# Cross attention's scores and maxima on two row tiles of the TensorE array

## The reference, cut to what matters

```python
x = _layernorm(x + attn(x))                       # self attention, 16 heads of 16
# cross attention: x (32, 112, 256) over ctx (32, 375, 256)
q1, q2 = (q[..., :8], q[..., 8:])                 # each of the 16 heads has two halves of 8
k1, k2 = (k[..., :8], k[..., 8:])
a1 = softmax(q1 @ k1.T / sqrt(8)); a2 = softmax(q2 @ k2.T / sqrt(8))
attn_output = (a1 - lam * a2) @ v                 # times 0.8, out projection
x = _layernorm(x + output)
x = x + moe(x)                                    # 8 experts, top 2, then a last norm
```

## Time and profile before

| | |
|---|---|
| median of 3 runs | 1861.12 us |
| the profiled execution's own time | 1862.62 us |
| its span, first to last instruction | 1860.7 us |
| TensorE busy (modelled) | 1629.8 us, 88% |
| VectorE busy | 1153.1 us, 62% |
| ScalarE busy | 915.8 us, 49% |
| mean granted TensorE clock | 0.954 |
| cross attention, first to last score matmul | 479.4 to 1183.8 us |

### The profile page before, as it was taken

How to read it: one execution, slowest core, us unless ns; L and a number is a source line. 1 busy time by engine, 2 the same in 40 slices (tenths; PEclk the granted TensorE clock), 3 DMA queues, 4 the chain that set the end, 5 groups by cost and what they waited for, 6 DMA issues and landing times. The chain is left out here.

```text
span 1860.7 us, 46590 instructions
## 1 busy us (share of the span) xinstructions
PE 1629.8 (88%) x17724; PEld 1223.2 (66%) x17724; DVE 1153.1 (62%) x2648; ACT 915.8 (49%) x2168; POOL 747.5 (40%) x928
## 2 busy tenths in 40 slices
PE   4899999995999999999999998579999999999950
PEld 2666666663566666666665665368888888888840
DVE  5566666662888887788777888434444444444424
ACT  2344444443466666666666665434444444444423
POOL 6343343322755666765775576301111101111116
PEclk9999999997799999999999999779999999999985
DMA  6666666644444445555554453356555566666637
GB/s 174 186 188 172 177 187 176 181 112 97 136 139 138 131 125 145 145 140 136 147 166 124 132 150 98 127 199 238 224 220 222 223 228 237 238 238 228 220 88 184
DMA packets 204149, 317.11 MB, mean 170 GB/s; under 512 B 60600, under 2 KB 170840, under 8 KB 203928
## 3 DMA queue, kind: packets, MB, share of 16 engines
q1 hardware_dynamic: 188280, 247.16, 44.5%
q0 software_dynamic: 15648, 66.97, 10.2%
HBM read 225.84 MB, written 87.89 MB: 169 GB/s over the span
## 5 line engine op out<-in xcount | busy, mean ns | idle before, releaser
L1165 DVE TENSOR_REDUCE cross_mx<-cross_bank_max 112x2 f32<-112x750 f32 x512 | 460.7, 933 | 119.1 <-PE cross_bank_max L1245 116.4
L996 ACT ACTIVATE cross_probs<-cross_bank_score 125x448 f32<-125x448 f32 x768 | 406.5, 545 | 241.9 <-PE cross_bank_score L1235 238.9
L1556 PE MATMUL experts_bank_h<-experts_x_hi,w 128*128 128x256 f16 x2240 | 373.3, 274 | 1.4 <-DVE experts_x_lo L1477 1.4
L1556 PE MATMUL experts_bank_h<-experts_x_lo,w 128*128 128x256 f16 x1120 | 306.6, 274 | 0.0
L1514 DVE TENSOR_TENSOR experts_hid<-experts_bank_h,experts_gated 128x256 f32<-128x256 f32 x280 | 118.6, 424 | 285.5 <-ACT experts_gated L1453 285.4
L1235 PE MATMUL cross_bank_score<-cqst,ckst 97*125 97x448 f16 x768 | 283.9, 371 | 4.8 <-ACT cross_probs L996 2.4
L1245 PE MATMUL cross_bank_max<-ckst,cqst 96*112 96x375 f16 x1024 | 258.8, 335 | 28.2 <-DVE cross_mx L1165 21.2
L1427 POOL DMA_INDIRECT y<-experts_y,experts_dest_i x70 | 67.2, 960 | 510.1 <-ACT experts_y L1465 499.4
L1556 PEld LDWEIGHTS experts_bank_h<-experts_x_hi,w 128*128 128x128 f16 x2240 | 220.0, 98 | 27.7 <-DVE experts_x_lo L1477 1.8
L1261 PE MATMUL cross_bank_out<-cross_probs,cross_val 125*32 125x112 f32 x6144 | 202.0, 264 | 0.1
L1453 ACT ACTIVATE experts_gated<-experts_bank_h 128x256 f32<-128x256 f32 x280 | 107.5, 384 | 189.9 <-PE experts_bank_h L1556 185.5
(11 more groups left out here) (216 smaller groups left out, 2746.9 us busy)
## 6 DMA issues: line engine op xcount, KB each, us to landing
w<-w_halves SPq DMA_DIRECT2D x35, 3072.0 KB, 11.7
cross_ew<-in_experts POOLq DMA_DIRECT2D x32, 768.0 KB, 5.5
w_halves<-cross_ew_half POOLq DMA_DIRECT2D x32, 768.0 KB
ckst<-cross_k SPq DMA_DIRECT2D x96, 187.5 KB
cross_v<-front_v SPq DMA_DIRECT2D x24, 531.2 KB
cross_val<-cross_v SPq DMA_DIRECT2D x32, 398.4 KB
front_src<-in_ctx_t SPq DMA_DIRECT2D x24, 500.0 KB, 8.9
experts_rows<-routed SPq DMA_DIRECT2D x35, 260.0 KB, 6.3
```

The source lines that it names most:

```text
L996: nc.scalar.activation(probs[:, e % PROBS], bank_score[e % 2][0:SC, 0:4 * T], ACT.Exp, scale=CROSS_SCALE).then_inc(probs_ready, 1)
L1165: nc.vector.tensor_reduce(mx[:, b % nb, 2 * n:2 * n + 2], bank_max[n % 2][0:T, :, 0:S], AX.X, ALU.max).then_inc(max_read, 1)
L1556: last = nc.tensor.matmul(bank_h[f % 4][:, mat * BLOCK:(mat + 1) * BLOCK], w13(p, wh, mat, k, f), xt[:, p, k], start=n == 0, stop=n == len ...
```

## The change

Each group's 96 rows are cut in two tiles of 64 rows of the array: head j of the two has its 3 terms x 16 channels = 48 rows at partitions 64 j to 64 j + 47, and a row of ones (in `kst`) or of negated maxima (in `qst`) at 64 j + 48. `qst` has now 2 x 112 columns for a group in place of 4 x 112. A score part becomes two matmuls of 49 rows x 224 columns, one on each tile, both into the same bank. A maxima matmul has 48 rows and 375 columns as before. The pair of maxima of the odd n is cut: its tile-1 half moves to part k = 1, its tile-0 half stays at k = 2. The second score of each part waits on a new semaphore `half_full` until the first is complete. The maxima's order in `mx` is kept by `units_of`. The keys come in 6 transfers of 16 channels in place of 3 of 32, and each row of maxima in two transfers of 8 units in place of one of 16.

```diff
-        sp.dma_start(kst[32 * term:32 * term + 32, p],
-                     cross_k[half].rearrange("(g r) n -> r g n", r=32)[:, :, bass.ts(b, S)]).then_inc(sem, 16)
+        src = cross_k[half].rearrange("(g j r) n -> j r g n", j=2, r=16)
+        for j in range(2):
+            row = 64 * j + 16 * term
+            sp.dma_start(kst[row:row + 16, p], src[j, :, :, bass.ts(b, S)]).then_inc(sem, 16)
...
-            row = 32 * term + 8 * i
-            sp.dma_start(qst[row:row + 8, p, :, i * T:(i + 1) * T], src[i, :, :, bass.ts(b, T)]).then_inc(sem, 16)
+            row = 64 * (i // 2) + 16 * term + 8 * (i % 2)
+            sp.dma_start(qst[row:row + 8, p, :, (i % 2) * T:(i % 2 + 1) * T], src[i, :, :, bass.ts(b, T)]).then_inc(sem, 16)
...
-                pool.memset(ckst[STACK:STACK + 1], 1.0).then_inc(early_ones, 1)
+                pool.memset(ckst[:], 1.0).then_inc(early_ones, 1)
...
-                    sp.dma_start(qst[STACK:STACK + 1, p, 4 * h:4 * h + 4, :].rearrange("o g (i t) -> o (g i) t", t=T),
-                                 neg_mx[:, p, h]).then_inc(row_loaded[h][p], 16)
+                    for j in range(2):
+                        at = 64 * j + TILE_ROWS
+                        sp.dma_start(qst[at:at + 1, p, 4 * h:4 * h + 4, :].rearrange("o g (i t) -> o (g i) t", t=T),
+                                     neg_mx[8 * j:8 * j + 8, p, h]).then_inc(row_loaded[h][p], 16)
...
-                    for i in range(2):
-                        u = 2 * n + i
-                        last = nc.tensor.matmul(bank_max[n % 2][0:T, i, 0:S], qst[0:STACK, p, u // 4, (u % 4) * T:(u % 4 + 1) * T],
-                                                kst[0:STACK, p, u // 4, :], start=True, stop=True)
-                    last.then_inc(max_full, 1)
+                def score(b, e, j):
+                    g, k = divmod(e, CHUNKS)
+                    p = b % nb
+                    rows = slice(64 * j, 64 * j + TILE_ROWS + 1)
+                    return nc.tensor.matmul(bank_score[e % 2][0:SC, 2 * j * T:2 * (j + 1) * T], kst[rows, p, g, k * SC:(k + 1) * SC],
+                                            qst[rows, p, g, :], start=True, stop=True)
+                def maximum(b, n, j):
+                    g, i = divmod(n, 2)
...
+                    if j == 1:
+                        wait(pe, max_read, 2 * GROUPS * b + n - 1)
+                    rows = slice(64 * j, 64 * j + TILE_ROWS)
+                    return nc.tensor.matmul(bank_max[n % 2][0:T, j, 0:S], qst[rows, p, g, i * T:(i + 1) * T],
+                                            kst[rows, p, g, :], start=True, stop=True)
+                def scores_and_maxima(c, e):
+                    b, (g, k) = c + lead, divmod(e, CHUNKS)
+                    first_tile = 1 if k == 2 else 0
+                    if on(c):
+                        before_scores(c, e)
+                        score(c, e, first_tile).then_inc(half_full, 1)
+                    if on(b):
+                        if k == 0:
+                            maximum(b, 2 * g, 1)
+                            maximum(b, 2 * g, 0).then_inc(max_full, 1)
+                        elif k == 1:
+                            maximum(b, 2 * g + 1, 1)
+                        else:
+                            maximum(b, 2 * g + 1, 0).then_inc(max_full, 1)
+                    if on(c):
+                        wait(pe, half_full, PARTS * c + e + 1)
+                        score(c, e, 1 - first_tile).then_inc(scores_full, 1)
...
-                        if on(c):
-                            scores(c, e)
-                        if k != 1 and on(c + lead):
-                            maxima(c + lead, 2 * g + k // 2)
+                        scores_and_maxima(c, e)
```

More of the change, by code:

```diff
@@ L126 @@
 CROSS_RING = 3
+TILE_ROWS = 16 * TERMS
 CHUNK = 4
@@ L357, in _ @@
                         wait(sp, early_zeros, 1)
+                        wait(sp, early_ones, 1)
                         for b in range(2):
@@ L810, in cross @@
         row_loaded = [ph.sems(f"row_loaded{h}_", nb) for h in range(2)]
-        max_full, max_read, scores_full, probs_ready, probs_used = (ph.sem(s) for s in (
-            "max_full", "max_read", "scores_full", "probs_ready", "probs_used"))
+        max_full, max_read, half_full, scores_full, probs_ready, probs_used = (ph.sem(s) for s in (
+            "max_full", "max_read", "half_full", "scores_full", "probs_ready", "probs_used"))
         out_read = ph.sems("out_read", 2)
@@ L828, in cross @@
         consts = 7
-        loads = 16 * TERMS * 5
+        loads = 16 * TERMS * 6
         stacks_loaded = lambda b: loads * (b // nb + (0 if b % nb < 2 else 1))
@@ L976, in step_read @@
                         h = int(name[-1])
-                        wait(act, row_loaded[h][p], 16 * (b // nb))
+                        wait(act, row_loaded[h][p], 32 * (b // nb))
                         nc.scalar.activation(neg_mx[:, p, h], bank[0:16, 0:T], ACT.Copy, scale=-1.0).then_inc(read[name], 1)
@@ L1225, in _, with before_scores @@
                 pe.wait_ge(ident_ready, 5)
-                def scores(b, e):
-                    g, k = divmod(e, CHUNKS)
+                def before_scores(b, e):
                     p = b % nb
@@ L1232, in scores @@
                     if e % (PARTS // 2) == 0:
-                        wait(pe, row_loaded[e // (PARTS // 2)][p], 16 * (b // nb + 1))
+                        wait(pe, row_loaded[e // (PARTS // 2)][p], 32 * (b // nb + 1))
                     wait(pe, probs_ready, PARTS * b + e - 1)
-                    nc.tensor.matmul(bank_score[e % 2][0:SC, 0:pair_w], kst[:, p, g, k * SC:(k + 1) * SC], qst[:, p, g, :],
-                                     start=True, stop=True).then_inc(scores_full, 1)
-                def maxima(b, n):
+                def score(b, e, j):
+                    g, k = divmod(e, CHUNKS)
@@ L1247, in maxima @@
-                    last.then_inc(max_full, 1)
+                    rows = slice(64 * j, 64 * j + TILE_ROWS + 1)
[4 more added lines that the diff above has]
+                    p = b % nb
+                    if n == 0 and j == 1:
+                        wait(pe, loaded[p], stacks_loaded(b))
+                    if j == 1:
[3 more added lines that the diff above has]
+                                            kst[rows, p, g, :], start=True, stop=True)
@@ L1667, in decoder @@
         y = dram("y", [3 * NT + BLOCKS * BLOCK, D], F32)
-        ckst = ctx.enter_context(nc.sbuf_tensor("ckst", [STACK + 1, CROSS_RING, PAIRS, S], F16))
-        cqst = ctx.enter_context(nc.sbuf_tensor("cqst", [STACK + 1, CROSS_RING, PAIRS, 4 * T], F16))
+        ckst = ctx.enter_context(nc.sbuf_tensor("ckst", [64 + TILE_ROWS + 1, CROSS_RING, PAIRS, S], F16))
+        cqst = ctx.enter_context(nc.sbuf_tensor("cqst", [64 + TILE_ROWS + 1, CROSS_RING, PAIRS, 2 * T], F16))
         table_i = ctx.enter_context(nc.sbuf_tensor("table_i", [128, 2, BLOCKS], I32))
```

8 lines of the change are left out of this document (3 added, 5 removed).

## The result

The changed kernel takes 2326.86 us (four runs, 2325.26 to 2327.95) against 1862.42 us for the kernel before in the same comparison: a ratio of 1.249 [1.247, 1.252]. It is slower by 464 us. The prediction was slower, 1973 us, 1898 to 2022: the sign was right, the size was missed by a factor of four.

The account below looks back on a forecast made before the run. TensorE was taken to set the pace; with the change, new waits give eight groups of 2.60 us, plus steps, form changes and normalisations: 25.1 us a batch against 21.57, +112 us, so 1973 us, range 1898 to 2022.

Parts of the forecast that it names:

- a group of 2.60 us: Cross attention: a group of three parts without a step takes 2.60 us, against 2.06 before.
- rival 3: Scores and maxima: the tiles don't run side by side, streams are serial; + 18 us, 1991; chance 0.12.
- the form of the array: Steps between scores: changing the array's form costs 0.15 us behind each of three steps in k = 1, 0.45 a batch.
- The reading of row1's row: Steps: row1's transpose showed no gap, so no step would pay for form; 24.05 us a batch, 1939 us.
- the edits at nothing: Five more transfers a batch, setting ckst and cqst at the start, and the reduce's strided output: no cost.
- The moved wait (the largest term): Part k = 1, ahead of weigh: the moved half pair of maxima waits for VectorE's reading; round of 2.59 us.
- ScalarE's round: From k = 2 to the next: half_full delays the second score, then exponential and scores of k = 1; 2.62 us.
- VectorE's normalisations: VectorE's extra work of 1.16 us each delays the next round, by about 0.45 and 0.1: 0.5 us together.
- rival 4: TensorE's clock falls to 1.2 GHz, streams in the round double; + 205 us if always, 2178; chance 0.06.
- The gain on offer: Scores and maxima on two tiles side by side need 0.6 us a group instead of 1.2; kernel can't collect it.
- Rival 1: TensorE's chain alone decides, only half_full counts; 2.22 us a group, 1940 us; chance 0.22 with main case at low prices.
- Rival 2: Round from k = 2 to k = 2: stall swallows TensorE's present waits; 21.0 us a batch, 1843; chance of faster 0.08.

Follow-up runs that it names:

- x6: Kernel before with all scores and maxima cut to rows 0 to 63, one 64-row tile, same order and waits; 2071.13 and 2110.79 us, the first 1.072.
- x5: Kernel before with all scores and maxima cut to rows 0 to 64, still in the 128-row form, same order and waits; 2042.03 us, 1.057.
- x1: Kernel before with one added wait in each part, for its own score matmul, ahead of weigh or the next part; 1967.43 us, 1.020.
- x9: Changed kernel with tiles filled up to 64 rows and the odd pair of maxima whole in k = 2 again; 2242.65 us, 1.166 of the kernel before.
- x17: Kernel before with scores and maxima on 48 rows of one tile, order of before; 2355.12 us, 1.265.
- x10: Kernel before with all scores and maxima on rows 0 to 47, one tile, serial, same order and waits; 2370.02 us, 1.232.
- x7: Changed kernel with each tile's rows filled up to 64 by zeros and ones, all else the same; 2210.39 us, 1.145 of the kernel before.
- x18: Changed kernel with tiles filled up to 64 rows, run on another chip; 2149.20 us, 1.155 of the kernel before.
- x3: Kernel before with scores on the tile from row 64, maxima on rows 0 to 63, no half_full wait, no maxima moved; 2065.98 us, 1.072.

## Why the prediction was wrong

**What held.** The sum for a batch at the full clock. The text had 25.1 us, the full-clock stretches show 24.92 and 24.82. Against 21.6 that is 3.3 us a batch, 106 us over 32; the text had +112. In its parts:
- a group of 2.60 us: 2.61 measured;
- the 0.36 us from the first score of k = 2 to its second: 0.41 foretold;
- the tiles side by side (rival 3): both start in the same hundredth of a microsecond, so that rival falls;
- the form of the array: 0.15 us for each of the three steps behind weigh, 0.14 measured (x6 against x5). The reading of row1's row, by which no step would pay, is answered too: row1 stood between matmuls of its own form there, and pays 0.09 us on either side in x6;
- the edits at nothing: the stages outside keep their times.

**What was mis-attributed within it.** "The moved wait (the largest term)" is worth 0.1 us a batch. The base of 2.60 is right through ScalarE's round and `half_full`, which the text had computed as the longer by 0.03 us and then put second. x1 shows what a wait for the score's completion costs by itself, 0.95 us a batch in the old order. That the total came within 0.2 us is in part luck, for two errors in the steps cancel. In x9's batch of 24.82 us, taken from weigh to weigh, the router's score costs 0.8 us in place of 0.2, since TensorE waits there for ScalarE:

```profile
1260.74 0.53 PE L1333 MATMUL cross_bank_step<-cross_gate_w,cross_y_t 128*112 128x8 f32 x4 [0.51 <-ACT cross_y_t L991]
```

and VectorE's normalisations cost almost nothing in place of 0.5.

**What failed: rival 4, "The clock falls", with a chance of 0.06 and a price of 205 us.** The main sum takes every term at the full clock and puts nothing for a fall; the fall was left to this rival, and both its numbers were wrong.
- *The chance.* The text took TensorE's busy share as the sign of whether the clock holds: full at 92%, 0.68 at 78%. But the change alters something no busy share shows: a matmul that used 97 or 96 of the array's rows uses 49 or 48. x17 and x10 show that this alone, with every wait and order of the kernel before, takes the steady clock to 0.52 to 0.54. x1 shows that the waits alone leave its mean at 0.93 to 1.00 down to the last three batches. x7 and x18 show that rows filled up with zeros and ones give part of it back in the changed kernel itself.
- *The price.* The text doubled only the three streams of the round (0.8 us a group, 6.4 a batch). Measured, 36.92 - 24.92 = 12.0 us a batch. Nearly everything that TensorE does is on the round's path once its clock is low: a maxima matmul is complete after 0.56 us in place of 0.32, a score after 0.44 in place of 0.26, weigh takes 1.28 in place of 0.72, out0 to the next score 1.04 in place of 0.44 (0.58 with the change of form at the full clock).

Together: 32 x 3.3 = 106 us for the order and its waits, and 32 x 12.0 = 384 us for the clock, 490 in all. Measured are 464. The 21.6 and the 36.92 are undisturbed batches. The means over the stage are 704 / 32 = 22.0 and 1165 / 32 = 36.4 (about a quarter of the changed kernel's batches take 35.6), and these give 461.

**The gain on offer.** The text named 0.6 us of streams a group and said that the kernel could not collect it. x3 shows the same without the waits: at the full clock 21.5 us a batch against 21.7. Rival 1 (TensorE's chain alone, 2.22 us a group) falls at the full clock, where a group takes 2.61 and the score of k = 1 is released by ScalarE; at the low clock TensorE's chain with `half_full` is what decides, since it is busy 98% and waits for no reduce between 560 and 1400 us. Rival 2 is excluded by 24.9.

What stays open: what makes the clock of the 65-row kernels fall and return within a stage, which part of the change's order costs clock beside the rows, whether the rows of each matmul count or their sum over time, and why some chips give the kernel before 1927 us in place of 1862.

## What to carry to other kernels

Before cutting a contraction onto row tiles, compare the rows in use per matmul, not only the streams and the busy share: here 97 rows held the full clock and 48 lost it, and half of the clock outweighed any overlap. Look at the granted clock of the stage first when a kernel is slower than its critical path explains, and price a low clock on all of TensorE's work that lies on the path, latencies included. When two waits end within 0.03 us of each other, removing one brings little: 0.1 us a batch here.

## What the runs showed of the hardware that was not expected

- The granted clock of a stage went with the rows of the array in use: 1.00 at 80 rows, 0.94 at 65, 0.54 at 48, with the same order of instructions on one chip. 65 rows in the 128-row form and 64 in the 64-row form behaved alike (0.78 and 0.76 in the same 200 us). The order of the instructions counts beside it: 0.71 with 64 rows in the change's order, 0.94 with 65 in the old one.
- A modelled busy share of 98% went with a clock of 0.51. The Trainium skill (TensorE: Matmul & The Clock Gate, Part 1: The HAM clock gate (the "warmup" mystery)) describes a clock gate that follows how busy the array has been. The rows here say that an engine shown as always busy can be held at the lower level.
- Rows that compute nothing raise it: 49 rows filled up to 64 took the clock from 0.51 to 0.71, and the time from 2327 to 2149 us.
- A step in the full form set between matmuls of the 64-row form cost 0.14 us behind weigh and 0.11 on average over the eight (x6 against x5), while two tiles of the same form started together.
